# A decision-tree stage that sorts its tokens into 32 groups instead of 128

## The reference, cut to what matters

```
for _ in range(DEPTH + 1):                      # DEPTH = 7, so 8 levels, 255 nodes
    score = einsum('td,td->t', flat_x, w1s[current]) + b1s[current]
    all_nodes.append(current); all_logits.append(score)
    choice = ((sign(score) + 1.0) / 2.0).astype(int32)
    current = current * 2 + choice + 1
path_weights = gelu(abs(logits), approximate=False)
for i in range(DEPTH + 1):
    t_i = einsum('td,tdo->to', flat_x, w2s[nodes_i]) + b2s[nodes_i]    # 64x64 matrix per node
    out = out + t_i * path_weights[:, i][:, None]
h = h + out                                     # flat_x is the layer norm of h
```

## Time and profile before

| | before |
|---|---|
| median of 3 runs | 4554.62 us (4553.16 to 4555.21) |
| profiled execution: time, span | 4554.57 us, 4552.8 us |
| tree stage in the span | from 3732.3 us to the end, 820 us |
| first score on DVE, end of chunk loop | 3822.05, 4040.6 |
| scatter | 4073.33 to 4162.9 |
| tile loop on DVE | 4171.22 to 4495.29 |
| busy over the whole span | PE 77%, DVE 63%, ACT 49%, POOL 18% |

### The profile page before, as it was taken

One profiled execution on the slowest core, in us unless ns is written; L12 is line 12 of the kernel. 1 busy time (PEld: TensorE's weight loads), 2 busy tenths in 40 slices (PEclk: granted clock), 3 DMA queues, 4 the chain that ended last, 5 costly groups with the idle time before them and its releaser, 6 DMA issues. The chain is left out here.

```text
span 4552.8 us, 64348 instructions
## 1 busy us (share of the span) xinstructions
PE 3500.5 (77%) x23423; PEld 1849.2 (41%) x23424; DVE 2879.0 (63%) x4681; ACT 2243.2 (49%) x4461; POOL 835.3 (18%) x912
## 2 busy tenths in 40 slices
PE   6549999999999999748788885799589742522775
PEld 5224444444444443323444433233277532422654
DVE  1528878888878888557777771444133333863995
ACT  1138888888888888535555553233233111310110
POOL 1310111011011101110000000443100020016773
PEclk7569999999999999869998896899789875766997
DMA  1030010101110010120000004332311227031113
GB/s 42 8 94 19 21 41 19 28 19 24 28 38 19 21 26 19 24 64 10 9 8 11 6 8 95 65 73 65 92 45 38 54 63 67 10 58 33 43 41 74
DMA packets 150528, 173.36 MB, mean 38 GB/s; under 512 B 109171, under 2 KB 132724, under 8 KB 142307
## 3 DMA queue, kind: packets, MB, share of 16 engines
q1 hardware_dynamic: 108732, 151.84, 15.2%
q10 hardware_dynamic: 33216, 9.28, 2.1%
q0 software_dynamic: 8320, 8.73, 0.6%
HBM read 89.61 MB, written 46.60 MB: 30 GB/s over the span
## 5 line engine op out<-in xcount | busy, mean ns | idle before, releaser
L970 DVE TENSOR_REDUCE att_NM<-att_ring 121x1 f32<-121x1024 f32 x1088 | 1252.1, 1217 | 314.2 <-PE att_ring L833 313.6
L905 ACT ACTIVATE att_ring<-att_ring,att_NM 121x1024 f32<-121x1024 f32 x1088 | 1194.4, 1124 | 114.9 <-DVE att_NM L970 114.0
L831 PE MATMUL att_ring<-att_q,att_k 64*121 64x512 f32 x2176 | 1167.7, 646 | 40.4 <-DVE att_Y L960 15.8
L833 PE MATMUL att_ring<-att_q,att_k 64*121 64x512 f32 x2176 | 1167.4, 646 | 0.0
L831 PEld LDWEIGHTS att_ring<-att_q,att_k 64*121 64x121 f32 x2176 | 346.5, 187 | 727.4 <-ACT att_ring L905 524.9
L1338 ACT ACTIVATE gqa_PT<-gqa_ring 121x484 f32<-121x484 f32 (+3 forms) x912 | 359.6, 449 | 201.0 <-PE gqa_ring L1265 134.4
L1382 DVE TENSOR_REDUCE gqa_NM<-gqa_ring 121x1 f32<-121x484 f32 (+1 forms) x720 | 374.8, 579 | 119.6 <-PE gqa_ring L1242 80.1
L833 PEld LDWEIGHTS att_ring<-att_q,att_k 64*121 64x121 f32 x2176 | 346.7, 187 | 0.0
L1265 PE MATMUL gqa_ring<-gqa_QS,gqa_KS 128*121 128x484 bf16 (+3 forms) x912 | 273.3, 331 | 36.0 <-ACT gqa_PT L1338 23.1
L2462 PE MATMUL tree_pY<-tree_W,tree_xT 128*128 x1536 | 223.4, 289 | 79.5 <-ACT tree_xT L2502 59.9
L1242 PE MATMUL gqa_ring<-gqa_KS,gqa_QS 128*121 128x484 bf16 (+1 forms) x720 | 251.6, 375 | 40.2 <-ACT gqa_PT L1338 19.1
(11 more groups left out here) (437 smaller groups left out, 5476.5 us busy)
## 6 DMA issues: line engine op xcount, KB each, us to landing
moe_xw<-route_weights SPq DMA_DIRECT2D x17, 968.0 KB, 7.2
att_k<-att_k SPq DMA_DIRECT2D x32, 512.2 KB, 6.2
att_q<-att_q SPq DMA_DIRECT2D x32, 512.2 KB, 8.3
sorted_x<-tree_Z ACTq DMA_DIRECT2D x16, 438.0 KB, 16.6
tree_xt<-sorted_x SPq DMA_DIRECT2D x24, 292.0 KB, 3.1
n_T<-h SPq DMA_DIRECT2D x16, 384.0 KB
by_freq<-stu_Yf SPq DMA_DIRECT2D x32, 160.0 KB
stu_YT<-by_freq SPq DMA_DIRECT2D x8, 640.0 KB, 5.5
```

Of the source, the lines that this page charges most:

```text
L831: nc.tensor.matmul(to[0:TT, 0:512], lo[0:64, par, TT * t:TT * t + TT], mlo[0:64, par, CK * ck:CK * ck + 512], start=True, stop=True)
L833: nc.tensor.matmul(to[0:TT, 512:1024], hi[64:128, par, TT * t:TT * t + TT], mhi[64:128, par, CK * ck + 512:CK * ck + 1024], start=True, st ...
L905: nc.scalar.activation(to[0:TT, :], to[0:TT, :], ACT.Exp, bias=NM[0:TT, turn % 2, g, ck:ck + 1], accum_out=SS[0:TT, turn % 2, g, ck:ck + 1 ...
L970: nc.vector.tensor_reduce(NM[0:TT, turn % 2, g, ck:ck + 1], slot("score", turn, n)[0:TT, :], AX.X, ALU.max, negate=True).then_inc(S["max_r ...
```

## The change

All of it is in `stage_tree`. The tokens are sorted by their node of level 5 (32 groups) instead of their leaf (128), so 96 tiles do instead of 192. The levels 0 to 5 are fixed in a group (three pairs of matrices, WP); of levels 6 and 7 all 2 + 4 nodes below the group's node are multiplied (WG), each token with 12 weights of which the ones off its path are zero. The row in `sorted_x` has 77 numbers. Besides this:

- The zeros are 8 DMAs with rows of 3696 bytes; the big clearing on POOL and the wait for DVE's Z0 are gone. Unused slots go by token number zero, and numbers are shifted by 121.
- The chunk loop is written out, chunks and scores are double-buffered, and the residual h is loaded and transposed in it, to HT. PE makes the scores of a chunk ahead of the counts of the one before.
- The loads of the second-layer weights are issued by SP between chunks 1 and 2.
- The comparison is fused into the descent (`scalar_tensor_tensor`), and the ranks are made for four tiles at a time on 32 groups.
- Gelu is applied once, after all chunks.
- In the tile loop ScalarE scales four of the twelve results (levels 7), DVE eight, and DVE adds in four steps.
- The tail loads the results in four pieces, adds and stores them.

The core of the diff:

```
-SLOT_TILES = 192
+SLOT_TILES = 96
...
-PAIRS = LEVELS // 2
-WEIGHTS = slice(64, 64 + LEVELS)
...
+PAIRS = 3
+WEIGHTS = slice(64, 64 + 12)
...
+                for c in range(NCHUNK):
+                    if c >= 2:
+                        sp.wait_ge(S["turned"], c - 1)
+                    sp.dma_start(xs[0:64, c % 2, :], xn[:, MC * c:MC * c + MC]).then_inc(S[f"x_staged{c % 2}"], 16)
...
+                    sp.dma_start(hs[:, c % 2, 0:real(c)], h_in[:, MC * c:MC * c + real(c)]).then_inc(S[f"h_staged{c % 2}"], 16)
+                    if c == 1:
+                        for v, rows in ((w2v, slice(0, 64)), (b2v, slice(64, 65))):
...
+                            for a in range(4):
+                                sp.dma_start(WG[rows, :, 2 + a, :], v[:, 4 * GROUPS - 1 + a:8 * GROUPS - 1:4, :]).then_inc(S["w2_loaded"], 16)
...
-                nc.gpsimd.memset(W2[64:128, :, :, :], 0.0).then_inc(S["w2_zeroed"], 1)
...
-                act.wait_ge(S["id_filled"], 1)
-                for k in range(SLOT_TILES // 12):
-                    act.dma_start(sorted_x.rearrange("(t p) c -> p t c", p=ST)[:, 12 * k:12 * k + 12, :], Z0[:, :, :]).then_inc(S["zeroed"], 16)
+                zv = sorted_x.rearrange("(p t) c -> p (t c)", p=128)
+                for k in range(NZ):
+                    act.dma_start(zv[:, ZW * k:ZW * k + ZW], Z0[:, :]).then_inc(S["zeroed"], 16)
...
-                    nc.vector.tensor_scalar(POS[:, :, :], SC[:, :, :], 0.0, None, ALU.is_gt)
-                    ch(nc.vector.tensor_scalar(NEG[:, :, :], SC[:, :, :], 0.0, None, ALU.is_le))
...
-                        nc.vector.tensor_tensor(dst[:, :, :, 0], ON[:, :, src], NEG[:, :, src], ALU.mult)
+                        nc.vector.scalar_tensor_tensor(out=dst[:, :, :, 0], in0=sc[:, :, src], scalar=0.0, in1=on[:, :, src], op0=ALU.is_le, op1=ALU.mult)
...
+                        nc.tensor.matmul(pL[:, j % 2, 0:256], xT[:, j % 2, :],
+                                         WG[:, bass.ds(g, 1), 2:6, :].rearrange("p a b o -> p (a b o)"), start=True, stop=True).then_inc(S["b_ready"], 1)
+                        pe.wait_ge(S["a_scaled"], 2 * TG * i + j - 1 + 2)
+                        nc.tensor.matmul(pA[:, j % 2, 128 * PAIRS:128 * PAIRS + 128], xT[:, j % 2, :],
+                                         WG[:, bass.ds(g, 1), 0:2, :].rearrange("p a b o -> p (a b o)"), start=True, stop=True)
...
+                        act.wait_ge(S["b_ready"], 2 * TG * i + j + 1)
+                        act.wait_ge(S["both_added"], 2 * TG * i + j - 1 + 2)
+                        for k in range(4):
+                            w = xt[:, j // TG, j % TG, 64 + 8 + k:64 + 9 + k]
+                            ins = nc.scalar.mul(pq[:, j % 2, k, :], pL[:, j % 2, 64 * k:64 * k + 64], w)
+                        ins.then_inc(S["b_scaled"], 1)
...
-                        nc.vector.tensor_reduce(yt[:, q, j % TG, :], pr[:, j % 2, :, :].rearrange("p l o -> p o l"), AX.X, ALU.add).then_inc(S["y_ready"], 1)
+                        nc.vector.tensor_tensor(half[:, :, :], pr[:, j % 2, 0:4, :], pr[:, j % 2, 4:8, :], ALU.add).then_inc(S["halved"], 1)
...
+                        nc.vector.tensor_tensor(both[:, :, :], half[:, :, :], pq[:, j % 2, :, :], ALU.add).then_inc(S["both_added"], 1)
...
+                        nc.vector.tensor_tensor(pair[:, :, :], both[:, 0:2, :], both[:, 2:4, :], ALU.add).then_inc(S["pair_added"], 1)
...
+                        nc.vector.tensor_tensor(yt[:, q, j % TG, :], pair[:, 0, :], pair[:, 1, :], ALU.add).then_inc(S["y_ready"], 1)
```

More of the change, by code:

```diff
@@ L2321, in stage_tree @@
-        BACK = [(0, 4), (4, 8), (8, 12), (12, NCHUNK)]
+        NINIT, NLOAD = 6, 16 * 5
+        NW2 = 6 * PAIRS + 12
+        BACK = [(17 * k, 17 * k + 17) for k in range(4)]
+        NLOOP = SLOT_TILES // (2 * TG)
+        real = lambda c: min(MC, B * N - MC * c)
         with nc.Block() as block:
@@ L2429, in _ @@
+                    for t in range(MK):
+                        ins = nc.tensor.transpose(pX[0:MT, 1, 64 * t:64 * t + 64], hs[:, i % 2, MT * t:MT * t + MT], C[0:64, 0:64])
+                    ins.then_inc(S["h_turned"], 1)
+                scores(0)
+                for i in range(NCHUNK):
+                    if i + 1 < NCHUNK:
+                        scores(i + 1)
                     pe.wait_ge(S["path_ready"], i + 1)
+                    nc.tensor.matmul(pP[0:MT, 0:32 * (MK + 1)], C[0:MT, 128 * BEFORE:128 * BEFORE + MT], ON[:, :, G0:G0 + GROUPS], start=True, stop=False)
@@ L2443, in _ @@
-                regs = [pe.alloc_register(f"node{k}") for k in range(PAIRS)]
-                with pe.Fori(0, SLOT_TILES // (2 * TG)) as i:
+                pe.wait_ge(S["w2_loaded"], 16 * NW2)
+                regs = [pe.alloc_register(f"node{k}") for k in range(PAIRS + 1)]
+                with pe.Fori(0, NLOOP) as i:
                     def turn(j):
@@ L2562, in _ @@
-                    for l in range(LEVELS):
+                        else:
+                            ch(ins)
+                    ch(nc.vector.tensor_tensor(PR[:, :, :], on, sc, ALU.mult))
+                    for l in range(LEVELS - 2):
                         w = 2 ** l
-                        ins = nc.vector.tensor_reduce(G8[:, :, l], PR[:, :, w - 1:2 * w - 1], AX.X, ALU.add, apply_absolute_value=True)
-                    ins.then_inc(S["g_raw"], 1)
-                    tiles = bass.ds(i * MK, MK)
@@ L2568, in _ @@
-                    nc.vector.tensor_scalar(O[:, tiles, :], ON[:, :, LEAVES - 1:NODES], 0.0, None, ALU.add)
-                    dve.wait_ge(S["counted"], i + 1)
-                    for t in range(MK):
-                        q = slice(128 * t, 128 * t + 128)
-                        ch(nc.vector.tensor_tensor(RA[:, :], pP[0:MT, q], CUM[0:MT, :], ALU.add))
-                        ch(nc.vector.scalar_tensor_tensor(out=RA[:, :], in0=RA[:, :], scalar=1.0, in1=ON[:, t, LEAVES - 1:NODES],
-                                                          op0=ALU.mult, op1=ALU.mult, accum_out=RK4[:, t:t + 1]))
-                        ch(nc.vector.tensor_tensor(CUM[:, :], CUM[:, :], pC[:, q], ALU.add))
@@ L2583, in _ @@
+                    ch(nc.vector.tensor_reduce(RK[:, tiles], RA[:, :, :], AX.X, ALU.add))
                 ch0(nc.vector.tensor_scalar(ti[:, :], CUM[:, :], float(ST - 1), None, ALU.add))
```

381 lines of the change are left out of this document (187 added, 194 removed).

## The result

The changed kernel takes **4310.8 us** (4309.4 to 4317.4, four runs), the one before 4554.9 (4553.2 to 4557.2): a ratio of 0.9467, with a 95% interval of 0.945 to 0.9483. That is 244 us less. The forecast was 4250 (304 less), its range 4218 to 4305: the direction was right, the time lies 5.8 us above the range. The profiled execution has a span of 4309.1 us, 60.7 more than the 4248.4 of the forecast's sum.

A forecast was written before the change was run, and what follows sets the result against it. The prediction took the stage as a chain of waits, with DVE leading in the chunk and tile loops. Its parts in sequence ended the tile loop at 4212.7; plus 2.7, tail 33 and 1.8 gave 4250 us, range 4218 to 4305.

The forecast's parts named there:

- PE's 1.7 us a tile: Tile loop: PE's transpose and pair products about 1.2 us, 256 more columns 0.47, together 1.7, under DVE's time.
- rival P: PE's clock stays low: a chunk takes 8.0 us and a tile 2.9, total 4335 us; chance 0.07.
- Start: Start of the stage: eight zero issues take 3 us, W1 copied at about 3740, DVE starts at about 3745, 77 us saved.
- Stall: Chunk 1: DVE waits some 27 us, as chunk 2's loads queue behind the weight loads; chunk 2 starts at 3788.6.
- C: Rival on the start: no stall, chunk 2 arrives in time, total 4223 us; chance 0.12.
- Chunk: Chunk loop: DVE leads with 7.15 us a chunk, where it was 12.8; 15 chunks from 3788.6 take 107.3 us.
- Slots, scatter, first product: After the chunks: slots 6.5 us; scatter 1.05 to its start, then 91.26; first product 6.63 plus 0.95.
- Tile on DVE: Tile loop: DVE leads with 2.14 us a tile, 96 tiles 205.4 us, 210.4 with extras, against 324 before.
- Tail: After the tile loop: from the loads to the end 33 us, between 27.8 and 40, against 54.9 before.
- POOL and DVE (G): Rival in the tile loop: DVE's additions wait for POOL's store, 0.85 us a tile, total 4332 us; chance 0.07.
- Serial hand-overs (S): Rival: a tile's hand-overs between PE, ScalarE and DVE don't overlap, 6.4 us a tile, total 4663 us; chance 0.02.

The follow-up runs named there:

- experiment 2: The changed kernel with xs and W1 given 128 rows (65 to 127 zero) for the chunk loop's scores, tile loop left at 65 rows: 4304.7 us, ratio 0.9453.
- experiment 1: The changed kernel with xT, WP and WG given 128 rows in the tile loop, rows 65 to 127 zero: 4258.5 us, ratio 0.936.
- experiment 4: The kernel before the change, with its tile loop's four pair products reading 65 rows in place of 128: 4614.1 us, ratio 1.0116.
- experiment 3: The changed kernel, still 65 rows, with the tile loop's 256-column product split into two of 128 columns: 4316.6 us, ratio 0.9483.
- experiment 7: The changed kernel with xT, WP and WG at 128 rows, but WP's products reading 65 of them: 4266.1 us, one run.
- experiment 5: The changed kernel with the 30 weight loads issued behind the last chunk's loads in place of behind chunk 1's: 4289.0 us, ratio 0.9424.
- experiment 6: The changed kernel with 128 rows in the tile loop, 128 rows for the chunk loop's scores, and weight loads behind the last chunk's: 4230.9 us, ratio 0.9273.

## Why the prediction was wrong

**The failed step is PE's 1.7 us a tile, "under DVE", in the part on a tile**, with the sentence against rival P: a clock of 1.00 at 75% busy, "where it will be 80%". It carried the clock of the earlier trace rows over to products of another shape. The diff showed xT, WP and WG with 65 rows; I took them for less zeroing and priced the products alone. At the low level, 0.50, PE took 2.77 a tile and led. The tile loop is 58.1 of the 60.7 us, and 55.3 of these come back with 128 rows (271.2 to 215.9); the other 2.8 are DVE's tile. In the chunk loop the same cause costs some 5 more (experiment 2). Experiments 1 and 4 show it both ways, and 3 and 7 take away the other candidates. Rival P was what came true, with a chance of 0.07; it names no cause for the low clock. Its price of 4335 was 24 too high, since it multiplied PE's whole time by 1.7, where the tile came to 2.77 for 2.9, the chunk to 7.68 for 8.0, and the tail was shorter.

The other steps:
- **Start:** DVE at 3748.9 for 3745, 4 late. The eight issues of zeros took ScalarE's queue 8.91 us for the "3 us" of the forecast, and W1 was copied behind them, at 3743.56 for 3740.
- **Stall:** 22.5 us in chunk 1 and 2.2 in chunk 0, for "some 27"; chunk 2 at 3788.37 for 3788.6. The weight loads cause it (experiment 5), and C, no stall, falls. That the end of the loads came out to 0.1 us, 39.3 us for 39.4, is luck in part: the sum had 13.3 for the zeros beside the weights, which cost about 5 (39.3 less the 34.5 of experiment 5), and nothing for the issue of the 15 small bias loads, which took SP 10.4 us (3766.31 to 3776.69), in the last 5 us of them with the DMA engines nearly idle, at a share of 0.05.
- **Chunk:** 7.68 for 7.15, 7 us in all. Of the 0.53, PE at the low clock is 0.38 (experiment 2). Of the rest, the reduces take 0.28 more than forecast (1.05 us for the 512 strided numbers), and the copy and ranks 0.13 less. The fused operation costs what the plain product did, 427 ns for 256 numbers.
- **Slots, scatter, first product:** 6.5, 92.2 and 7.5 us for 6.5, 92.3 and 7.6.
- **Tile on DVE:** forecast 2.14, and 215.9 / 96 = 2.25 with the loop's ends when the clock is up. The gap ahead of the addition of both halves, which waits for two engines, is 0.1 (6.1 / 64 in experiment 1) where I had 0.035. ScalarE's scalings take 314 ns each in the mean, but they overlap: the four of a tile take 0.93 us together, 0.23 each, within the bound of "at most 0.26".
- **Tail:** 28.5 us from the loads to the end for 33. The lower end of the forecast, 27.8, adds up to 27.4 from its own terms; the 33 doesn't rest on it.
- **POOL and DVE (G):** refuted by experiment 1: 0.06 us for some additions, not 0.85 a tile. The Trainium skill's "GPSIMD Engine Reference", section "Key points", says that GpSimd contends with VectorE instructions that run in a 2-port perf mode or have two SBUF inputs. For the second kind, beside the issue of an indirect store the trace shows next to nothing of it, 426 ns an addition beside 1007 ns issues. What did hold DVE here was a clearing; the operation that it held, a `tensor_scalar`, has one SBUF tensor and a column of scalars as inputs, and whether it is of the first kind no row shows.
- **Serial hand-overs (S):** a tile takes 2.77 us, and not 6.4; the engines overlap.

With the edits of experiments 1, 2 and 5 together, which take away the low clock in both loops and the stall, the kernel comes to 4230.9, below the forecast of 4250, since the forecast held the stall.

## What to carry to other kernels

When a change alters the shape of TensorE's products, do not carry the granted clock over from the profile before: price them at both levels, and look in the diff for the number of rows that they read. Rows of zeros that look like waste can be worth their clearing; here 15 us of clearing on GpSimd buy 55 us in the tile loop. The clearing belongs where VectorE has nothing to do: one held an operation of VectorE for its whole length (10.34 us in experiment 1), and cost 2.2 us in experiment 6. And when loads move ahead in a queue, name the first small load behind them and who waits for it.

## What the runs showed of the hardware

TensorE was granted the low level for 269 us on end while 99% busy with products of 65 rows (the transposes among them read 128, and did not lift it), and the full one at 87% busy with 128 rows, half of them zeros. The Trainium skill's page "TensorE: Matmul & The Clock Gate", in its "Part 1: The HAM clock gate", puts the level down to how busy PE has been recently; by the busy time of the profile alone that is not what these two rows show. A mixture of both kinds ran at 1.00 after its first tiles (experiment 7), and at 0.77 where only a chunk's scores were padded (experiment 2). Nor is it the rows of a single product. The attention stage of the same trace makes its scores from products of 64 rows, at 1.00:

```profile
L831 PE MATMUL att_ring<-att_q,att_k 64*121 64x512 f32 x2176 | 1166.6, 646 | 40.1 <-DVE att_Y L960 16.1
...
L833 PE MATMUL att_ring<-att_q,att_k 64*121 64x512 f32 x2176 | 1166.4, 646 | 0.0
```

```profile
1501.30:1504.50 3.20, 3.20 (x17) 1.38 (x16) 2.06 (x2) 2.85 (x5) 0.00 (x0) 1.00 0.00 0
```

There they come in pairs, L831 on rows 0 to 63 and L833 on rows 64 to 127, that start within 0.01 us of each other, so that both together span 128 rows. What the chip counts stays open: the runs tell that rows bear on the level, not how, and no kernel was run with a number between 65 and 128 in the tile loop.
